# Rows of maxima in two halves, 16 unread products, and another order of parts behind the head slots

## What is computed

```python
x = x + attn_a(layernorm(x), Wq, Wk, Wv, bq, bk, bv, Wo, bo)   # 16 heads of 64, causal
x = x + ffn(layernorm(x), w1, b1, w2, b2)                       # width 512, relu
x = x + attn_b(layernorm(x), W_qk, W_v, alibi_slope)            # one head of 128, causal, linear bias
x = x + ffn(layernorm(x), w1, b1, w2, b2)                       # the same weights
```

## Time and profile before

| | |
|---|---|
| time, median of 3 runs | 578.79 us (577.55 to 579.03) |
| the profiled execution's own time | 579.0 us |
| its span, first to last instruction | 577.0 us |
| mean granted TensorE clock | 0.988 |
| PE busy | 528.2 us, 92% |
| DVE busy | 444.7 us, 77% |
| ACT busy | 468.5 us, 81% |
| POOL busy | 455.8 us, 79% |
| chain that ended last | PE 65%, ACT 10%, DVE 9%, issue 8%, POOL 7%, DMA 1% |

### The profile page before, as it was taken

How to read it: one execution, slowest core, us unless ns; L and a number is a source line. 1 busy time by engine, 2 the same in 40 slices (tenths; PEclk the granted TensorE clock), 3 DMA queues, 4 the chain that set the end, 5 groups by cost and what they waited for, 6 DMA issues and landing times.

```text
span 577.0 us, 17876 instructions
## 1 busy us (share of the span) xinstructions
PE 528.2 (92%) x6844; PEld 369.8 (64%) x6844; DVE 444.7 (77%) x1383; ACT 468.5 (81%) x923; POOL 455.8 (79%) x446
## 2 busy tenths in 40 slices
PE   4688999899999999999999999997988998788886
PEld 3445666566676667666766667664788795546664
DVE  5588888788888888888888888887776575689822
ACT  3659889889988999899989999889873869473983
POOL 5658899678888888888888888896965956564995
PEclk9989999999999999999999999999989999899999
DMA  9423334232433333423334243358108000000001
GB/s 230 113 56 72 85 86 111 56 94 58 119 84 94 93 76 102 104 74 96 80 104 110 56 121 77 100 141 319 39 38 292 2 3 2 1 1 2 1 20 55
DMA packets 36435, 48.54 MB, mean 84 GB/s; under 512 B 10728, under 2 KB 17792, under 8 KB 36352
## 3 DMA queue, kind: packets, MB, share of 16 engines
q1 hardware_dynamic: 34240, 46.88, 29.6%
q10 hardware_dynamic: 2112, 0.54, 0.4%
HBM read 12.79 MB, written 9.44 MB: 39 GB/s over the span
## 4 chain that ended last, share of the span: by engine, by line
PE 65%; ACT 10%; DVE 9%; issue 8%; POOL 7%; DMA 1%; POOLq 0%; ACTq 0%; DVEq 0%
PE psum L555 9%; PE psum L611 9%; PE psum L612 9%; PE psum L509 6%; PE psum L511 6%; PE psum L510 6%; PE psum L591 5%; PE psum L593 5%; PE psum L592 5%; PE psum L614 2%; ACT xn L1130 2%; ACT p_hl L1202 2%; POOL h_lo L2077 2%; POOL p_hlb L2084 2%; POOL p_hl L2004 2%
## 5 line engine op out<-in xcount | busy, mean ns | idle before, releaser
L2004 POOL TENSOR_TENSOR p_hl<-p,p_hl 128x512 f16<-128x512 f32 x288 | 327.4, 1162 | 54.0 <-ACT p_hl L1202 50.6
L1481 DVE CUSTOM_DVE_ANT_0 max_junk<-psum,mask_s 128x1024 bf16<-128x1024 f32 (+7 forms) x256 | 190.2, 753 | 32.0 <-issue 31.8
L1201 ACT ACTIVATE p<-psum 128x512 f32<-128x512 f32 x288 | 178.2, 619 | 16.4 <-PE psum L614 14.1
L1202 ACT ACTIVATE p_hl<-psum 128x512 f16<-128x512 f32 x288 | 179.6, 624 | 0.0
L591 PE MATMUL psum<-v_all,p_hl 128*128 128x65 f16 x1152 | 125.5, 193 | 1.7 <-POOL p_hl L2004 1.7
L611 PE MATMUL psum<-q_hl,k_hh 128*128 128x512 f16 (+3 forms) x384 | 125.1, 326 | 1.4 <-ACT p_hl L1202 1.4
L592 PE MATMUL psum<-v_all,p_hl 128*128 128x64 f16 x1152 | 125.6, 193 | 0.0
L593 PE MATMUL psum<-v_all,p_hl 128*128 128x65 f16 x1152 | 125.2, 194 | 0.0
L612 PE MATMUL psum<-q_hm,k_l 128*128 128x512 f16 (+3 forms) x384 | 121.8, 326 | 0.0
L591 PEld LDWEIGHTS psum<-v_all,p_hl 128*128 128x128 f16 x1152 | 107.4, 98 | 16.7 <-POOL p_hl L2004 1.8
L592 PEld LDWEIGHTS psum<-v_all,p_hl 128*128 128x128 f16 x1152 | 106.7, 97 | 4.9
(11 more groups left out here) (205 smaller groups left out, 1109.1 us busy)
## 6 DMA issues: line engine op xcount, KB each, us to landing
k_hh<-st_hi SPq DMA_DIRECT2D x64, 128.0 KB, 2.3
o_scratch<-o_sb SPq DMA_DIRECT2D x16, 512.0 KB, 2.6
o_in<-o_scratch SPq DMA_DIRECT2D x4, 2048.0 KB, 10.5
k_l<-st_lo SPq DMA_DIRECT2D x32, 128.0 KB, 2.3
q_hl<-st_hi SPq DMA_DIRECT2D x32, 128.0 KB, 2.3
q_hl<-st_lo SPq DMA_DIRECT2D x32, 128.0 KB, 2.3
q_hm<-st_hi SPq DMA_DIRECT2D x32, 128.0 KB, 2.3
x_sb<-in_L_attn_a_x SPq DMA_DIRECT2D x4, 256.0 KB, 3.7
```

The costliest lines, as they stand in the source:

```text
L1201: nc.scalar.activation(p32[:, ring_at(u, r), :], src, ACT.Exp, scale=SCALE_A).then_inc(exp_done, 1)
L1202: nc.scalar.activation(p_hl[:, u % 2, 0, BANK * r:BANK * (r + 1)], src, ACT.Exp, scale=SCALE_A).then_inc(phi_done, 1)
L1481: nc.vector.tensor_tensor_reduce(out=max_junk[:, n % 2, 0:cols], in0=max_banks(v, j, 0, cols), in1=mask_s[:, S - cols:S], scale=1.0, scala ...
L2004: nc.gpsimd.tensor_tensor(p_hl[:, u % 2, 1, cols], p32[:, ring_at(u, r), :], p_hl[:, u % 2, 0, cols], ALU.subtract)\
```

## The change

1. **Rows of maxima in two halves.** max_rows_b makes qm_b by two operations on 8 x 512 (four of the eight rows of queries each) instead of one on 8 x 1024, each with an increment of mrowb_done. scores_b waits for the first half at unit 0 and for the second at unit 2; the other waits on that semaphore count double.
2. **16 products.** Ahead of the first scores of batch 0, PE issues 16 products of 128x128 that nothing reads, behind the other waits of that unit and ahead of the wait for the rows of maxima.
3. **Another order of parts.** The lists of PE, ACT, DVE and POOL behind the slots have the same parts in another order. SP's list stays. The places that the text below speaks of are in the excerpt.

```diff
@@ PE, turn_late and turn_maxima_b: the waits on mrowb_done count double
                 if n == ln_of[2, 2]:
-                    pe.wait_ge(mrowb_done, 1)
+                    pe.wait_ge(mrowb_done, 2)
...
@@ PE, scores_b
                 if r == 0:
-                    pe.wait_ge(mrowb_done, b + 1)
                     pe.wait_ge(qb_lo_done, 2 * (b + 1))
                     pe.wait_ge(k_one_ready, 2)
                     if b == 0:
                         pe.wait_ge(h_hi_done, FW * CHUNKS)
+                        idle_products(16, S_BANKS[0][0])
                     else:
                         pe.wait_ge(maxb_done, QT * B)
+                    pe.wait_ge(mrowb_done, 2 * b + 1)
+                if r == 2:
+                    pe.wait_ge(mrowb_done, 2 * b + 2)
...
@@ PE, the list behind the slots
             turn_block(0, 0)
             turn_block(0, 1)
+            outputs(HEADS - 1, 0)
             turn_block(0, 2)
-            outputs(HEADS - 1, 0)
-            outputs(HEADS - 1, 1)
             turn_block(0, 3)
             turn_block(0, 4)
+            outputs(HEADS - 1, 1)
             turn_block(0, 5)
             outputs(HEADS - 1, 2)
             turn_block(0, 6)
             outputs(HEADS - 1, 3)
             outputs(HEADS - 1, 4)
-            outputs(HEADS - 1, 5)
             turn_block(0, 7)
             turn_block(1, 0)
+            outputs(HEADS - 1, 5)
             outputs(HEADS - 1, 6)
...
             output_tile(1, 0)
             output_tile(1, 1)
+            turn_late(ln_of[1, 0])
             output_tile(1, 2)
             output_tile(1, 3)
-            turn_late(ln_of[1, 0])
...
             forward(1, 3)
+            hidden(2, 0)
+            hidden(2, 1)
             output_tile(3, 0)
+            output_tile(3, 1)
             turn_late(ln_of[2, 0])
-            output_tile(3, 1)
             output_tile(3, 2)
             output_tile(3, 3)
+            hidden(2, 2)
             queries_b(0)
             turn_late(ln_of[2, 1])
-            hidden(2, 0)
-            hidden(2, 1)
+            hidden(2, 3)
             values_b(0)
-            hidden(2, 2)
             queries_b(1)
+            forward(2, 0)
+            forward(2, 1)
+            max_tile_b(0, 0)
             turn_late(ln_of[1, 3])
...
             forward(3, 1)
-            max_tile_b(0, 5)
+            max_tile_b(0, 7)
             forward(3, 2)
             forward(3, 3)
-            max_tile_b(0, 6)
-            max_tile_b(0, 7)
             turn_maxima_b(0)
             scores_b(0, 0)
...
+            forward(6, 0)
             hidden(7, 3)
-            forward(6, 0)
@@ ACT
             exponentials(HEADS - 1, 6)
-            tail_high(0)
+            exponentials(HEADS - 1, 7)
             block_high(0, 0)
             block_high(0, 1)
             block_high(0, 2)
-            exponentials(HEADS - 1, 7)
+            exponentials(HEADS - 1, 8)
             block_high(0, 3)
             block_high(0, 4)
-            exponentials(HEADS - 1, 8)
             block_high(0, 5)
+            tail_high(0)
...
             exponentials_b(0, 0)
+            late_norm(ln_of[2, 3])
             queries_high(2)
@@ DVE
                 dve.wait_ge(mtb_full, b + 1)
                 dve.wait_ge(rows_b, 1)
-                nc.vector.tensor_tensor(qm_b[0:QT, b, :].rearrange("p (j q) -> p j q", j=QT),
-                                        bank(LB)[0:QT, 0:P].unsqueeze(1).to_broadcast([QT, QT, P]),
-                                        neg_diag[:, :].unsqueeze(2).to_broadcast([QT, QT, P]), ALU.mult).then_inc(mrowb_done, 1)
+                for j in range(0, QT, CT):
+                    nc.vector.tensor_tensor(qm_b[0:QT, b, P * j:P * (j + CT)].rearrange("p (j q) -> p j q", j=CT),
+                                            bank(LB)[0:QT, 0:P].unsqueeze(1).to_broadcast([QT, CT, P]),
+                                            neg_diag[:, j:j + CT].unsqueeze(2).to_broadcast([QT, CT, P]), ALU.mult).then_inc(mrowb_done, 1)
...
+            outputs_out(HEADS - 2, 0)
             tail_norm()
-            tail_gain()
-            outputs_out(HEADS - 2, 0)
             outputs_out(HEADS - 2, 1)
             block_low(0, 0)
             block_low(0, 1)
             block_low(0, 2)
-            tail_low(0)
+            tail_gain()
             block_low(0, 3)
-            outputs_out(HEADS - 1, 0)
             block_low(0, 4)
             block_low(0, 5)
+            tail_low(0)
...
             block_low(1, 5)
+            add_result(0, 1)
+            late_stats(ln_of[1, 0])
             block_low(1, 6)
-            add_result(0, 1)
             block_low(1, 7)
-            late_stats(ln_of[1, 0])
...
+            chunk_low(ln_of[1, 2])
             add_result(4, 0)
-            block_low(3, 6)
             block_low(3, 7)
             add_result(4, 1)
...
+            max_rows_b(0)
             late_stats(ln_of[2, 3])
-            max_rows_b(0)
...
+            outputs_out_b(0, 2)
+            max_rows_b(1)
             outputs_out_b(0, 3)
-            max_rows_b(1)
+            biased(1, 0)
+            biased(1, 1)
+            outputs_out_b(0, 4)
             late_stats(ln_of[3, 0])
-            biased(1, 0)
@@ POOL
-            tail_root()
             low(HEADS - 1, 0)
             low(HEADS - 1, 1)
             low(HEADS - 1, 2)
             low(HEADS - 1, 3)
             low(HEADS - 1, 4)
+            tail_root()
             low(HEADS - 1, 5)
-            add_output_row(0)
...
-            late_rstd(ln_of[1, 2])
             late_rstd(ln_of[2, 0])
+            add_forward_row(1)
             late_rstd(ln_of[2, 1])
...
+            low_b(1, 0)
+            low_b(1, 1)
             late_rstd(ln_of[3, 0])
-            low_b(1, 0)
-            add_forward_row(4)
...
+            hidden_low(7, 3)
             add_forward_row(7)
-            hidden_low(7, 3)
```

More of the change, by code:

```diff
@@ L1082, in _ @@
             outputs_b(1, 7)
+            hidden(5, 2)
             turn_late(ln_of[3, 2])
-            hidden(5, 2)
             forward(4, 0)
+            hidden(5, 3)
+            hidden(6, 0)
             forward(4, 1)
-            hidden(5, 3)
             forward(4, 2)
             forward(4, 3)
-            hidden(6, 0)
+            turn_late(ln_of[3, 3])
             hidden(6, 1)
+            forward(5, 0)
             hidden(6, 2)
-            forward(5, 0)
             forward(5, 1)
-            turn_late(ln_of[3, 3])
             hidden(6, 3)
             forward(5, 2)
+            hidden(7, 0)
             forward(5, 3)
-            hidden(7, 0)
             hidden(7, 1)
             hidden(7, 2)
+            forward(6, 0)
             hidden(7, 3)
-            forward(6, 0)
             forward(6, 1)
@@ L1405, in _ @@
             hidden_high(4, 1)
-            late_norm(ln_of[3, 1])
             hidden_high(4, 2)
@@ L1846, in _ @@
             values_low(0)
+            add_result(6, 0)
+            take_max_b(0, 0)
+            chunk_low(ln_of[1, 3])
+            take_max_b(0, 1)
             queries_low(1)
-            chunk_low(ln_of[1, 3])
-            take_max_b(0, 0)
-            values_low(1)
-            take_max_b(0, 1)
-            add_result(6, 0)
-            take_max_b(0, 2)
-            add_result(6, 1)
-            take_max_b(0, 3)
-            late_stats(ln_of[2, 2])
-            take_max_b(0, 4)
+            add_result(6, 1)
+            take_max_b(0, 2)
+            late_stats(ln_of[2, 2])
+            take_max_b(0, 3)
+            take_max_b(0, 4)
+            take_max_b(0, 5)
+            take_max_b(0, 6)
+            values_low(1)
             add_result(7, 0)
-            take_max_b(0, 5)
+            take_max_b(0, 7)
             add_result(7, 1)
-            take_max_b(0, 6)
-            take_max_b(0, 7)
+            max_rows_b(0)
             late_stats(ln_of[2, 3])
-            max_rows_b(0)
             biased(0, 0)
+            biased(0, 1)
             chunk_low(ln_of[2, 2])
-            biased(0, 1)
             biased(0, 2)
+            biased(0, 3)
             queries_low(2)
-            biased(0, 3)
             biased(0, 4)
             chunk_low(ln_of[2, 3])
+            values_low(2)
             biased(0, 5)
-            values_low(2)
             biased(0, 6)
-            biased(0, 7)
             queries_low(3)
             take_max_b(1, 0)
+            biased(0, 7)
             biased(0, 8)
+            take_max_b(1, 1)
             values_low(3)
-            take_max_b(1, 1)
+            take_max_b(1, 2)
             outputs_out_b(0, 0)
-            take_max_b(1, 2)
+            take_max_b(1, 3)
             outputs_out_b(0, 1)
-            take_max_b(1, 3)
-            outputs_out_b(0, 2)
             take_max_b(1, 4)
@@ L2126, in _ @@
             hidden_low(1, 3)
-            late_rstd(ln_of[1, 2])
             late_rstd(ln_of[2, 0])
+            add_forward_row(1)
             late_rstd(ln_of[2, 1])
-            steps_masked(1)
-            late_rstd(ln_of[1, 3])
+            add_forward_row(2)
```

(17 more changed lines are left out.)

198 lines of the change are left out of this document (98 added, 100 removed).

## The result

The changed kernel takes 578.52 us (median of 22 runs, 576.72 to 581.07), the kernel before 576.55 beside it (22 runs, 574.62 to 580.20). The ratio is 1.0036, with a 95% interval of 1.0019 to 1.0054: slower by 2.0 us, where 2.8 less were forecast. The profiled execution of after took 578.36 us with a span of 576.6 and a mean granted clock of 0.985. That of before, 579.0 us and 0.988, was one of its longer ones: of 23 runs of before in a later comparison the 14 with a mean clock of 0.990 or more took 574.5 to 578.0, the other nine 577.7 to 579.8. No run of after had more than 0.988.

What follows compares the result with a forecast made beforehand. Waits between in-order queues were taken to bound the kernel, PE being full from 450 to 470 us and POOL tightest from 528.04 to 571.36. +2.7 ahead of E and -5.5 behind it gave -2.8: 576.2 us, range 572.5 to 580.0.

Steps and rivals of the forecast that it cites:

- the clock behind the wait: After PE's wait at turn_block(0, 6): 1.2 GHz loses 1.7 to 3.0 us, against 1.7 before; 0.6 more taken.
- the rest ahead of E: From the result tiles to E: +0.8 at output_tile(1, 0), -1.2 for waits of 0.72 and 0.44 that go.
- E: The end of forward(3, 3) on PE, 497.50 us in the kernel before; forecast to move by +2.7 us.
- the base: The profiled execution the sum starts from: 579.0 us, span 577.0, taken as 0.2 above the median of 578.79.
- tail_gain behind block_low(0, 2): DVE's seven steps wait for POOL, so PE waits 4.1 us ahead of turn_block(0, 6); result tiles start 3.1 late.
- taken at 0, bounds -1.5 to +2: Ahead of E: hidden(2, ...) fills PE, but the later chain hidden(3), h_lo, forward(3) costs it back; 0 us net.
- From E to the first scores: add_result(7, 1) 0.5, then half a row 0.65: scores start at E + 1.2, 2.2 us earlier; the clock holds.
- First pass: b = 0: last exponential at E + 17.5, rows of maxima b = 1 at E + 23.2, exponentials(1, 0) at E + 25.85.
- Second pass: POOL starts low_b(1, 0) at E + 26.9; last h_lo ends at E + 68.3, before E + 73.9: 5.5 us less.
- the first (no stall): Ahead of turn_block(0, 6): POOL is through or takes turns fast, so 3.1 goes: -5.9, 573.1 us; chance 0.18.
- the second: At the first scores: the products do not hold the clock, scores run at 1.2 GHz: -0.4, 578.6 us; chance 0.21.
- the third: Cross-wait at add_forward_row(1): 4.3 us lie open ahead of output_tile(3, 0): +2.2, 581.2 us; chance 0.14.

Runs made afterwards that it cites:

- e7: The changed kernel, but POOL waits for tail_gain to be done before low part 6 of the last head: 575.55 us, ratio 0.9981 to the kernel before.
- e4: The kernel before with only the two halves of rows of maxima and the 16 products, old order everywhere: 577.33 us, ratio 0.9998 to the kernel before.
- e5: The order of the kernel before up to E and the changed order behind it, halves and products kept: 572.48 us, ratio 0.9927 to the kernel before.
- e14: The changed kernel with 64 products that nothing reads ahead of turn_block(0, 6): 576.59 us, ratio 0.9979 to the kernel before.
- e1b: The same kernel as e1, run once more: 573.08 us, ratio 0.9923 to the kernel before.
- e15: e1 with add_forward_row(7) ahead of hidden_low(7, 3) on POOL again: 574.21 us, ratio 0.9954 to the kernel before.
- e16: e1 with late_rstd(3, 0) ahead of low_b(1, 0) on POOL again: 574.50 us, ratio 0.9958 to the kernel before.
- e10: e1 without the 16 products ahead of the first scores: 573.66 us, ratio 0.9943 to the kernel before.
- e1: The changed kernel with tail_root, tail_gain and outputs_out(30, 0) back in their old places: 572.81 us, ratio 0.9933 to the kernel before.
- e17: e1 with late_stats(2, 3) ahead of the rows of maxima of b = 0 on DVE again: 573.43 us, ratio 0.9941 to the kernel before.
- e6: The changed order up to E and the order of the kernel before behind it, halves and products kept: 582.11 us, ratio 1.0080 to the kernel before.

## Why the prediction was wrong

Two terms of the sum failed in size: the 0.6 us for the clock behind the wait ahead of turn_block(0, 6), and the -0.4 us for the rest ahead of E. With them failed the base, an execution with two falls of the clock that were taken for the kernel's.

- **tail_gain behind block_low(0, 2): right in mechanism and length.** Wait 3.95 (forecast 4.1), at 426.01 (426.25), output_tile(0, 0) 3.3 later (3.1), and four long steps again beside POOL's operations (the last two, with POOL nearly through, took 0.15 and 0.14); e7 shows the cause.
- **The clock behind the wait: the size was wrong.** "A loss of 1.7 to 3.0, against the 1.7 of before. I take 0.6 more." The fall at 425.0 to 428.4 was one of that execution of before. The profiles of e4 and e5, with its order there, have none between 412 and 430, and half of before's runs (49 of 97 in the four comparisons) have a mean clock of 0.990 or more, which after never reaches. From turn_block(0, 6) to output_tile(0, 0) it is 4.1 us in e4 and e14, at full clock, 5.8 in the profile of before and 6.9 in that of after. So the fall costs 2.8, inside the recorded 1.7 to 3.0; against the profiled execution 1.1 of it is new, not 0.6, and against one of before without the fall all of it. Likewise the fall at the first scores, which the change was credited with ending, is worth nothing by the medians when the products alone are added (e4).
- **"The rest ahead of E", taken at -0.4: wrong by 1.9 us.** E came 4.8 later, not 2.7: 3.3 up to output_tile(0, 0) and 1.5 behind it. The 0.72 went, but of the 0.44 there are 0.36 left; the wait at output_tile(1, 0) grew by 1.0, as 0.8 was forecast; and the 0.96 of the last maxima is not hidden: waits of 0.63 and 0.23 for maxima stand in front of the last forward tiles instead. The part "taken at 0, bounds -1.5 to +2" came out at +1.1: PE's waits from 470 us to E are 3.3 us before and 4.4 now. Besides, the fall of the clock behind the longer wait at output_tile(1, 0), 1.6 us in half of the profiles, had no term; it is not in the profile of after.
- **From E to the first scores: right.** E + 1.17 (forecast 1.2), the two halves 0.64 each (0.65), no fall of the clock there.
- **First pass: right, with one miss.** Last exponential at E + 17.7 (17.5), rows of maxima b = 1 at E + 23.8 (23.2), but exponentials(1, 0) at E + 27.2 (25.85). The clock was at 0.50 from 521.0 to 527.5: this fall was not in the forecast. In e1b, where it does not come, low_b(1, 0) starts at E + 26.9, which is the forecast.
- **Second pass: right in mechanism, and in its sum by luck.** h_lo ends at E + 68.6 (68.3), but low_b(1, 0) starts at E + 28.5, 1.6 late, and from there it is 40.1 us, 38.6 busy, where 41.4 were forecast: nearly all of the 1.4 us left for waits for ACT are gone. In e1b both come without the fall, and h_lo ends at E + 67.1. The last wait of PE is 0.65 (before 1.30). e15 and e16 confirm that the row of 1.23 and the place of late_rstd(3, 0) lie on the path.
- **The base.** The sum was made on an execution of 579.0 us whose kernel has a median of 576.55 beside after. Its two slow stretches were taken as properties of the kernel. So of the 4.8 us between forecast (-2.8) and result (+2.0), about half is in the profiled pair (-0.4 of span against -2.8: the middle) and half is the base, which I put down to the clock. Executions in which the clock did not fall from the first turn_block on bear this out: to PE's end it is 153.4 us in e4 (the old order), 152.3 in e14 and 149.4 in e1b, against 156.7 in after and 156.8 in before. So the new order with its stall would be 1.1 us ahead of the old one, were it not for the 2.8 of the fall behind the stall and the 1.6 of the one at b = 1.
- **The bounds.** Added up, those of the terms ahead of E (-0.6 and +0.7, -1.5 and +2) give 574.1 to 578.9 us, not 574.3 to 578.3.

Of the rivals, the first (no stall) falls by the wait of 3.95; the second by the clock at the first scores, which holds with the products (after) and without them (e10), so that its -0.4 of span and 578.6 us, which are nearly what was measured, are met by chance; the third by its place: there is no wait of more than 0.2 us ahead of output_tile(3, 0). The slower result came from the forecast's own mechanism at a higher price. What stays open is what decides, from one execution to the next, whether the clock falls at the gaps of 0.3 to 2.2 us, and whether PE's own order makes the wait at output_tile(1, 0) longer, which was not tried.

## What to carry to other kernels

Before a small operation is moved in an in-order list, look at what runs on the engine that it has to wait for, and at what is queued behind it at the new place: here seven steps worth 0.8 us held DVE for 4.9 us. A fall of the clock in one profile is a property of that execution until several runs show it; compare the mean clock of all runs first, and price a long gap of PE with the clock behind it, 2 to 3 us here for a gap of 4, and 1.6 us in half of the profiles for one of 2.2. When a wait in front of one tile is to be hidden by moving its producer, count the new waits at the place it goes to.

## What the runs showed of the hardware

- DVE operations on 128x5 to 128x1 elements take 0.14 to 0.22 us with POOL idle (e7). Beside POOL operations of 1.12 to 1.24 us that follow each other closely, four of the seven took 1.08 to 1.31 us in after and five 1.07 to 1.20 in before. The slope step, on 128x1, took 0.20 beside them and 0.21 without them.
- Executions of one kernel on one chip spread over 4 to 5 us (e1, before), and the time follows the mean granted clock: e1 took 570.7 and 570.8 at 0.997, 571.5 to 572.8 at 0.994, 573.7 at 0.991 and 573.7 to 575.1 at 0.985 to 0.988.
- The gap of 1.15 us ahead of the first scores left the clock at 1.00 (e10), and so did one of 1.46 with 16 products ahead of it (e17) and one of 2.01 (e7). Behind one of 1.68 it fell (before), behind one of 2.19 it fell in six of twelve profiles, and behind that of 3.95 in both (after, e6).
- Two DVE operations on 8x512 take 1.27 us together (after), one on 8x1024 takes 1.18 (before): halving the columns nearly halves this form.
